# Window attention on one core: the third group of the next batch's tokens is turned in word 28 instead of word 27

## Reference

```python
h = h + _L1_attn_ref(_layernorm(h, axis=-1), wq, wk, wv, wproj, bproj, rk_v, rk_h, rv_v, rv_h)

B, N, E = x.shape                       # 4, 750, 192; 12 heads of 64
q = (x @ wq).reshape(B, N, H, HD).transpose(0, 2, 1, 3)
attn = jnp.einsum('bhid,bhjd->bhij', q, k) * scale
attn = attn + jnp.einsum('bhid,ijd->bhij', q, rpk) * scale
attn = jax.nn.softmax(attn, axis=-1)
out = jnp.einsum('bhij,bhjd->bhid', attn, v)
out = out + jnp.einsum('bhij,ijd->bhid', attn, rpv)
return out.transpose(0, 2, 1, 3).reshape(B, N, H * HD) @ wproj + bproj
```

## Time and profile before

| | us |
|---|---|
| three runs, median | 1837.29 |
| lowest and highest of them | 1833.49 and 1843.19 |
| the profiled execution | 1845.31 |
| its span, first to last instruction | 1843.6 |
| mean granted TensorE clock in the span | 0.895 |
| PE / weight loads / DVE / ACT / GpSimd busy | 85% / 80% / 65% / 54% / 19% |

### The profile page before, as it was taken

How to read it: one execution, slowest core, us unless ns; L and a number is a source line. 1 busy time by engine, 2 the same in 40 slices (tenths; PEclk the granted TensorE clock), 3 DMA queues, 4 the chain that set the end, 5 groups by cost and what they waited for, 6 DMA issues and landing times. The chain is left out here.

```text
span 1843.6 us, 32271 instructions
## 1 busy us (share of the span) xinstructions
PE 1575.8 (85%) x10779; PEld 1476.3 (80%) x10780; DVE 1190.7 (65%) x2207; ACT 1000.7 (54%) x1781; POOL 350.5 (19%) x495
## 2 busy tenths in 40 slices
PE   5864599983699999899899899899999899648993
PEld 4764588873599899899899899899899898538993
DVE  3588555546686786786687686687786686562333
ACT  4134133323578577678578678578578577233330
POOL 4040366652010010010010010010010010213441
PEclk6875699996899899999899999899999899658997
DMA  5034011118010010110010110010010100441114
GB/s 192 16 80 136 22 55 52 55 50 209 17 50 10 27 51 10 29 50 10 27 50 10 29 48 12 28 42 18 28 42 18 28 8 18 128 166 34 43 42 116
DMA packets 66847, 94.72 MB, mean 51 GB/s; under 512 B 17824, under 2 KB 52338, under 8 KB 66330
## 3 DMA queue, kind: packets, MB, share of 16 engines
q1 hardware_dynamic: 58026, 75.19, 14.0%
q0 software_dynamic: 8688, 17.80, 3.4%
HBM read 71.71 MB, written 21.06 MB: 50 GB/s over the span
## 5 line engine op out<-in xcount | busy, mean ns | idle before, releaser
L2471 DVE TENSOR_TENSOR a_Plo<-a_PT,a_Phi 125x756 fp32r<-125x756 f32 x288 | 281.8, 979 | 72.5 <-ACT a_PT L2196 71.4
L2196 ACT ACTIVATE a_Phi<-a_S 125x756 fp32r<-125x756 f32 x288 | 231.2, 803 | 156.8 <-PE a_O L1990 128.8
L2361 DVE TENSOR_REDUCE a_nmx<-a_M 125x1 f32<-125x752 f32 x248 | 232.7, 938 | 108.2 <-PE a_M L1865 107.1
L1685 POOL TENSOR_TENSOR a_qlo<-a_work,a_qhi 127x750 fp32r<-127x750 f32 x48 | 79.2, 1656 | 1019.3 <-PE a_S L1971 514.9
L2196 ACT ACTIVATE a_PT<-a_S 125x756 f32<-125x756 f32 x288 | 230.2, 799 | 0.0
L1023 PE MATMUL m_psG<-m_w,m_xT 128*128 x788 | 169.7, 355 | 5.4 <-DVE m_xT L1295 4.2
L1971 PE MATMUL a_S<-a_qhi,a_khi 128*125 128x378 f32 x576 | 154.0, 349 | 13.8 <-DMA a_qhi<-a_mrow 7.5
L1983 PE MATMUL a_O<-a_Phi,a_vhi 125*128 125x378 f32 x576 | 150.2, 342 | 1.4 <-issue 1.1
L1023 PEld LDWEIGHTS m_psG<-m_w,m_xT 128*128 128x128 f32 x788 | 138.7, 194 | 12.9 <-issue 11.5
L1971 PE MATMUL a_S<-a_qhi,a_klo 128*125 128x378 f32 x576 | 148.5, 339 | 0.0
L1971 PE MATMUL a_S<-a_qlo,a_khi 128*125 128x378 f32 x576 | 147.9, 338 | 0.0
(11 more groups left out here) (388 smaller groups left out, 3130.2 us busy)
## 6 DMA issues: line engine op xcount, KB each, us to landing
a_qhi<-a_rdens SPq DMA_DIRECT2D x48, 187.5 KB, 3.3
m_w<-in_m_w SPq DMA_DIRECT2D x16, 384.0 KB, 8.3
a_wkv<-a_w4k SPq DMA_DIRECT2D x8, 768.0 KB, 4.8
a_wq<-a_w4q SPq DMA_DIRECT2D x8, 768.0 KB, 6.3
a_wkv<-a_w4v SPq DMA_DIRECT2D x8, 768.0 KB, 5.9
a_qhi<-a_mrow SPq DMA_DIRECT2D x288, 0.5 KB
m_w<-in_m_w SPq DMA_DIRECT2D x8, 576.0 KB
m_X<-m_xn SPq DMA_DIRECT2D x8, 504.0 KB
```

Of the source, the lines that this page charges most:

```text
L1685: pool.tensor_tensor(qlo[0:ONE, u % HG % QLO, :], work[0:ONE, u % HG, 0:L], qhi[0:ONE, u % HG, :].bitcast(F32), ALU.subtract).then_inc(sg[ ...
L2196: last = nc.scalar.activation(to[:, wd % 2, :].rearrange("p (a l) -> p a l", a=2), psS[wd % 2][0:P, :, 0:HP], ACT.Exp, scale=SCALE)
L2361: v.tensor_reduce(nmx[:, u % 2, c:c + 1], bank[0:P, :, 0:376], AX.XY, ALU.max, negate=True).then_inc(sg["max_ready"], 1)
L2471: v.tensor_tensor(Plo[:, wd % 2, :], PT[:, wd % 2, :], Phi[:, wd % 2, :].bitcast(F32), ALU.subtract).then_inc(sg["exp_rest"], 1)
```

## The change

`turn_tokens`, `copy_tokens` and `split_tokens` of group 2 go from word 27 to word 28, with PE's wait for `columns_ready` 1. As ACT and DVE run `fill(x - 1)`, their share goes from the head of word 28 to the head of word 29. Nothing is added or removed.

```diff
@@ -1784,7 +1784,7 @@
                     if x == 26:
                         turn_tokens(i + 1, 0)
                         turn_tokens(i + 1, 1)
-                    elif x == 27:
+                    elif x == 28:
                         waiter(pe, i + 1)("columns_ready", 1)
                         turn_tokens(i + 1, 2)
                     elif 29 <= x < 33:
```

## The result

The changed kernel takes 1846.34 us (median of 22 runs, 1840.21 to 1854.25) against 1839.66 us for the kernel before (22 runs): ratio 1.0038, 95% interval 1.0024 to 1.0053, or 6.7 us (4.4 to 9.8) slower. The forecast was 6.1 us more than before, at 1843.4 us, and no change by more than 0.5% as the likeliest verdict. The profiled execution has a span of 1846.3 us.

What follows compares the result with a forecast made beforehand. PE was taken to bound the second halves (busy 112.63 of 117.00 us). A shift of 3.15 us plus 2.92 us for clock falls made 6.1 us, added to the 1837.3 us median: 1843.4 us, range 1835 to 1849.5.

Steps and rivals of the forecast that it cites:

- The shift: In word 29, at three places, PE's pause grows from 1.63 to 2.7 us: 1.05 us later each, 3.15 us.
- The clock: Behind the longer pauses PE's granted clock falls to 0.50 at two of three places, 1.46 us each: 2.9 us.
- A: Rival: PE's pause grows by 1.05 us, clock falls at one place or none; 1840.5 to 1841.9 us; chance 0.25.
- B: Rival: in words 29 to 33 the lower clock lasts 6.8 us a place; 11.9 us slower, 1849.2 us; chance 0.09.
- C: Rival: PE's pause goes and nothing replaces it, gaining 1.85 us at three places; 1831.7 us; chance 0.06.
- D: Rival: the pause only changes place, ACT or DVE reaching group 2 1 us sooner; 1837.3 us, no change; chance 0.08.

Runs made afterwards that it cites:

- (4): The changed kernel with its three pauses filled by 14 matmuls of no use ahead of keys part 0; ratios to the kernel before 0.9993 and 1.0014.
- (2): The kernel before with PE's and ACT's part of the change moved, DVE's left at the head of word 28; ratio to before 0.9995.
- (3): The changed kernel with the copy `sums_back` of word 28 put behind DVE's group 2; ratio to the kernel before 1.0038.
- 1: The kernel before with only PE's part of the change moved to word 28; three sets gave ratios of 0.9985, 0.9958 and 0.9989.
- 5: The kernel before with DVE's two operations for group 0 at word 27 cut into pieces; ratios 1.0016 with four pieces, 1.0046 with ten.

## Why the prediction was right

**The shift.** Predicted 1.05 us a place, from a replay with the rows' durations; the one place without a fall gives 1.06 us, the filled kernels 1.09. Keys part 0 itself starts 0.99 us later at the first place. The replay's own steps hold too: the transposes start 0.42 us ahead at 707.01 for the predicted 707.44, and keys part 0 at 712.78 for 712.84. DVE's order was taken away by itself and is worth 1.03 us (2), of which the copy makes 0.7 (3). ACT's order was taken away only together with it, and is worth 1.37 us then (1 against 2). One sentence of the prediction was wrong. It puts ACT's copies of group 2 on the path that sets the pause's end. By its own replay they end at 710.95 and DVE takes up the group at 711.87, and in the changed kernel they were 1.08 us early; the sum didn't use them.

**The clock.** Predicted 1.46 us a fall and two falls of three. Over three profiles of the changed kernel it fell at eight of nine places; the eight measure 11.12 to 11.42 us, 11.29 on the mean, 1.42 us over the ninth. So the price was right, and two of three was too low: 3 x 1.06 + 8/3 x 1.42 = 7.0 us, where the runs gave 6.7 (4.4 to 9.8), and 1.0036 and 1.0027 in the other two comparisons. The number of falls was a choice between none and three, with nothing in the rows of before on a pause of this length in word 29; that it came near is in part luck.

The eight differ by where the low stretch lies. The distance from word 20 to word 35 holds all of it: 43.28 us without a fall, 44.78 to 44.83 at the five places where the fall began at most 0.14 us ahead of the pause's end or behind it, and 44.59 to 44.62 at the three where 0.41 to 0.52 us of the low stretch lay in the pause, in which PE had nothing to do. That is 1.50 to 1.55 us a fall, and 1.31 to 1.34. The 11.12 us are a place where the low stretch outlasts the shorter distance.

**The absolute time.** The forecast of 1843.4 us is 2.9 us under the measured 1846.34. Of these 2.4 us are the kernel before, 1837.29 us by the three runs at hand and 1839.66 by 22, and 0.6 the change.

**The rivals.** A (shift only) is what the filled kernel does, 3.3 us, and what the changed kernel would do without the clock. B (a longer stay at the lower level) did not occur: each fall at the places lasted 3.41 us. (Its 4.8 us at the lower clock would be 4.7, by 1.46 us for 3.41.) C (the pause is simply gone) is almost what happens when only PE's part moves, 1.33 us a place of the 1.85 that it would be worth; the mechanism that I gave against it, group 2 behind the exponential of word 28, is what that kernel takes away. D would be the kernel of (2), 0.04 us a place.

**What stays open.** That a pause of about 2 us was followed by a fall at two of six places (3 and 5) and one of the same length not, in equal surroundings, is shown but not explained. Nor is length all: at the turn of the loop, between matmuls as dense, 24 of 28 pauses of 2.27 to 3.08 us in the fourteen profiles were followed by a fall, and one of 2.99 us was not (in the filled kernel); and between the halves, behind small matmuls, a fall began 0.13 us after a pause of only 1.07 us (PE's part alone, 1027.98 to 1029.05 us).

## What to carry to other kernels

Moving a step on one engine into an idle slot moves its partners on the others behind whatever they do in that slot: replay every queue by the rows, and move only the part whose engine waits. Here PE's part gains 1.3 us a place, and the partners' parts lose 2.4. A pause that grows by 1 us can cost more in clock than in length; where it can't be removed, try whether work of no use in the pause keeps the clock up, as in (4). With a spread of runs twice the effect, compare distances between the same two instructions in the profiles, not spans.

## What the runs showed that I had not expected

- How often the clock fell behind a pause at the three places, in otherwise dense matmuls: none of 6 at 1.62 to 1.65 us, 2 of 6 at 1.96 to 2.04, 11 of 12 at 2.64 to 2.80, each for 3.41 us at 0.50 and 1.3 to 1.55 us of lost time. This is a count for these places, and no threshold (see what stays open).
- Cutting a DVE operation of 250 columns in four costs 0.19 us, two fifths of the 0.47 us that I had worked out from the one-column instructions: the pieces overlap.
- At the turn of the loop over batches PE stands for 2.3 to 3.1 us, and matmuls put behind the turn don't fill it.
